# Starting the large SBUF tiles of a gated attention and ternary FFN kernel on multiples of 2048 bytes

## The reference

```python
x = x + tanh(g_xattn[0]) * xattn(layernorm(x), ctx_1024, ctx_1024, Wq, Wk, Wv, Wo, bo)
x = x + tanh(g_ffn[0]) * ffn(layernorm(x), w1_w, w1_s, w2_w, w2_s, h1_w, h1_s, h2_w, h2_s, w3_w, w3_s)

# xattn: 16 heads of 16, causal mask, softmax, concat @ Wo.T + bo
# ffn, with tlin(x, w, s) = (x @ w.T) * s and ternary weights w:
h = silu(tlin(x, w1_w, w1_s)) * tlin(x, w2_w, w2_s)      # 256 -> 1024
h = gelu(tlin(h, h1_w, h1_s))                            # 1024 -> 1024
h = gelu(tlin(h, h2_w, h2_s))                            # 1024 -> 1024
return tlin(h, w3_w, w3_s)                               # 1024 -> 256
```

## Time and profile before

| | |
|---|---|
| median of three runs | 1804.46 us |
| profiled execution | 1806.88 us |
| its span, first to last instruction | 1804.8 us |
| TensorE busy (PE, share of the span) | 1730.7 us (96%) |
| TensorE weight loads (PEld) | 1465.8 us (81%) |
| VectorE, ScalarE, GpSimd busy | 73%, 72%, 61% |
| granted TensorE clock, mean | 0.985 of full speed |
| DMA | 231.37 MB, mean 128 GB/s |

### The profile page before, as it was taken

The page is one execution under the profiler, slowest core; times in us unless marked ns, Lnnn a source line. Parts: engine busy times, 40 slices in busy tenths (PEclk is TensorE's granted clock), DMA queues, the critical chain, the costliest instruction groups (busy, mean ns, idle before and its releaser), DMA issues.

```text
span 1804.8 us, 39555 instructions
## 1 busy us (share of the span) xinstructions
PE 1730.7 (96%) x11014; PEld 1465.8 (81%) x11014; DVE 1321.6 (73%) x2803; ACT 1306.7 (72%) x3014; POOL 1106.8 (61%) x1646
## 2 busy tenths in 40 slices
PE   3399999999999999999999999999999999999998
PEld 2288888888888888888888888888888888888876
DVE  5767777777777777777777777777778777777764
ACT  3477777777777777777778777778777777777764
POOL 4666566567556567656567656656655656755652
PEclk8699999999999999999999999999999999999999
DMA  9944545544455544445554454554445554445420
GB/s 288 242 108 109 131 128 142 141 111 116 122 134 134 139 121 113 120 128 134 139 129 114 114 131 128 145 136 113 114 129 132 137 139 114 114 121 134 117 59 7
DMA packets 370970, 231.37 MB, mean 128 GB/s; under 512 B 283136, under 2 KB 340736, under 8 KB 369408
## 3 DMA queue, kind: packets, MB, share of 16 engines
q1 hardware_dynamic: 368784, 219.23, 47.7%
q10 hardware_dynamic: 2160, 11.81, 1.9%
HBM read 113.53 MB, written 41.94 MB: 86 GB/s over the span
## 4 chain that ended last, share of the span: by engine, by line
PE 91%; issue 2%; DMA 2%; POOL 2%; ACT 1%; DVE 1%; SPq 1%; POOLq 0%; DVEq 0%; ACTq 0%
PE ffn L976 71%; PE work L916 12%; PE s_bank L951 3%; PE pv L967 3%; PE work L1056 2%; DMA pT<-p_parts 1%; POOL p_parts L468 1%; POOL p_parts L466 1%; DMA aw<-in_attn_w 0%; DMA q<-q_saved 0%; POOL hb L513 0%; ACT probs L821 0%; SPq L360 0%; SPq L356 0%; POOL ha L508 0%
## 5 line engine op out<-in xcount | busy, mean ns | idle before, releaser
L976 PE MATMUL ffn<-hb,W 128*128 128x512 f32 x2048 | 512.2, 402 | 1.4 <-POOL hb L513 1.4
L976 PE MATMUL ffn<-ha,W 128*128 128x512 f32 x2048 | 492.1, 397 | 0.8 <-POOL ha L508 0.8
L658 DVE TENSOR_REDUCE full<-ffn 128x256 f32<-128x512 f32 x512 | 349.5, 688 | 194.1 <-PE ffn L976 194.1
L976 PEld LDWEIGHTS ffn<-ha,W 128*128 128x128 f32 x2048 | 379.4, 188 | 90.6 <-POOL ha L508 1.7
L976 PEld LDWEIGHTS ffn<-hb,W 128*128 128x128 f32 x2048 | 377.6, 188 | 86.3 <-POOL hb L513 2.3
L821 ACT ACTIVATE probs<-probs,exp_bias 128x128 f32<-128x128 f32 x1024 | 320.4, 390 | 50.8 <-POOL exp_bias L476 49.7
L468 POOL TENSOR_TENSOR p_parts<-probs,p_parts 128x512 f16<-128x512 f32 x256 | 300.4, 1173 | 20.5
L513 POOL TENSOR_TENSOR hb<-full,hb 128x256 fp32r<-128x256 f32 x256 | 187.3, 737 | 122.3 <-ACT full L839 116.5
L976 PE MATMUL ffn<-x2T_hi,W 128*128 128x256 f32 x1024 | 258.5, 287 | 1.4 <-DVE x2T_lo L754 0.9
L839 ACT ACTIVATE full<-full,cols 128x256 f32<-128x256 f32 x512 | 253.1, 494 | 0.0
L976 PE MATMUL ffn<-x2T_lo,W 128*128 128x256 f32 x1024 | 252.9, 284 | 0.0
(11 more groups left out here) (82 smaller groups left out, 2341.1 us busy)
## 6 DMA issues: line engine op xcount, KB each, us to landing
k<-k_saved SPq DMA_DIRECT2D x256, 128.0 KB, 2.8
q<-q_saved SPq DMA_DIRECT2D x256, 128.0 KB, 2.8
k_saved<-k_parts SPq DMA_DIRECT2D x32, 512.0 KB, 3.2
q_saved<-q_parts SPq DMA_DIRECT2D x32, 512.0 KB, 3.1
wnat<-in_ffn_w ACTq DMA_DIRECT2D x11, 1024.0 KB, 7.5
xT<-in_x_T SPq DMA_DIRECT2D x32, 256.0 KB, 3.3
cT<-in_ctx_T SPq DMA_DIRECT2D x32, 256.0 KB, 3.4
x_in<-in_x SPq DMA_DIRECT2D x32, 256.0 KB, 3.7
```

What stands on the lines that cost most here:

```text
L658: dve.tensor_reduce(full[:, m % 4], src[:].rearrange("p (a t) -> p t a", a=2), AX_X, ALU.add).then_inc(done, 1)
L976: return pe.matmul(dst, w, h, **flags)
```

## The change

All small tiles (statistics, biases, constants, and `vs`, which is 3136 bytes) are allocated first, then a filler `to_boundary` that nothing reads or writes, then the large tiles in their old order. The scratch region shrinks from 8192 to 4096 bytes. Scratch 4096, constants 128, small tiles 8800 and filler 1312 come to 14336 = 7 x 2048, and since all large tiles have sizes that are multiples of 2048, each of the tiles in the table above then starts on a multiple of 2048. The last byte moves from 228064 to 225280. No instruction, operand shape, wait, or order on any engine changes; only addresses in SBUF do.

```diff
+TO_BOUNDARY = 328
-        W = sb("W", [P, W_COLS], F32R)
-        aw = sb("aw", [P, 4, KE, E])
-        wq, wk, wv, woT = (aw[:, i] for i in range(4))
         ident = sb("ident", [P, P])
         causal = sb("causal", [P, P])
...
-        x_in = sb("x_in", [P, ROWS, E])
         stats = sb("stats", [P, ROWS, 6])
         moments = sb("moments", [P, ROWS, 2])
         var_eps = sb("var_eps", [P, ROWS])
         rstd = sb("rstd", [P, ROWS])
+        vs = sb("vs", [P, ROWS, H, VCOLS], BF16)
+        negmax = sb("negmax", [P, PSLOTS, 4])
+        exp_bias = sb("exp_bias", [P, PSLOTS, 4])
+        head_sum = sb("head_sum", [P, 2, PAIR, D])
+        rden = sb("rden", [P, ROWS, H])
...
+        wait_holder = sb("wait_holder", [P, 1])
+
+        to_boundary = sb("to_boundary", [P, TO_BOUNDARY])
+
+        W = sb("W", [P, W_COLS], F32R)
+        aw = sb("aw", [P, 4, KE, E])
+        wq, wk, wv, woT = (aw[:, i] for i in range(4))
+        x_in = sb("x_in", [P, ROWS, E])
         xres = sb("xres", [P, ROWS, E])
         xT = sb("xT", [P, KE, TOK])
         cT = sb("cT", [P, KE, TOK])
...
-    nc = bacc.Bacc("TRN2", target_bir_lowering=False, num_devices=1, dynamic_dma_scratch_size=8192)
+    nc = bacc.Bacc("TRN2", target_bir_lowering=False, num_devices=1, dynamic_dma_scratch_size=4096)
```

More of the change, by code:

```diff
@@ L99, in sem @@
             return ctx.enter_context(nc.semaphore(name))
-        W = sb("W", [P, W_COLS], F32R)
-        aw = sb("aw", [P, 4, KE, E])
-        wq, wk, wv, woT = (aw[:, i] for i in range(4))
+        COPIES = 4
+        PSLOTS = 4
+        TSLOTS = 2
         ident = sb("ident", [P, P])
@@ L128, in program @@
         rstd = sb("rstd", [P, ROWS])
+        vs = sb("vs", [P, ROWS, H, VCOLS], BF16)
[3 more added lines that the diff above has]
+        rden = sb("rden", [P, ROWS, H])
+        stats2 = sb("stats2", [P, ROWS, 6])
+        moments2 = sb("moments2", [P, ROWS, 2])
+        var_eps2 = sb("var_eps2", [P, ROWS])
+        rstd2 = sb("rstd2", [P, ROWS])
+        wait_holder = sb("wait_holder", [P, 1])
[4 more added lines that the diff above has]
+        x_in = sb("x_in", [P, ROWS, E])
         xres = sb("xres", [P, ROWS, E])
@@ L131, in program @@
         cT = sb("cT", [P, KE, TOK])
-        COPIES = 4
         q_parts = sb("q_parts", [P, 2, ROWS, KE, P], F32R)
@@ L139, in program @@
         k_saved = nc.dram_tensor("k_saved", [2, ROWS, P, KE * P], F32, kind="Internal").ap()
-        vs = sb("vs", [P, ROWS, H, VCOLS], BF16)
         v_rest = sb("v_rest", [P, ROWS, E])
-        PSLOTS = 4
         probs = sb("probs", [P, PSLOTS, 4, P])
-        negmax = sb("negmax", [P, PSLOTS, 4])
-        exp_bias = sb("exp_bias", [P, PSLOTS, 4])
         p_parts = sb("p_parts", [P, 2, 2, 4, P], F16)
-        TSLOTS = 2
         pT = sb("pT", [P, TSLOTS, 2, 4, P], F16)
-        head_sum = sb("head_sum", [P, 2, PAIR, D])
-        rden = sb("rden", [P, ROWS, H])
         heads = sb("heads", [P, ROWS, E])
@@ L154, in program @@
         x1_prev = sb("x1_prev", [P, ROWS, E])
[L155 to L158, removed]
         x2n = sb("x2n", [P, ROWS, E])
-        wait_holder = sb("wait_holder", [P, 1])
         x2T_hi = sb("x2T_hi", [P, KE, TOK], F32R)
```

## The result

The changed kernel takes 1791.35 us in the median of four runs (1788.92 to 1793.29), the kernel before 1805.5 us in the median of four (1802.91 to 1808.18). The ratio is 0.992, with a 95% interval of 0.9901 to 0.9939: faster by 0.8%. The forecast was no difference, 1804.5 us.

A forecast was written before the change was run, and what follows sets the result against it. Blocks were taken as bound by matmul count times start distance, after a prologue mostly on DMA. All terms were 0 (0 + 0 + 0 + 0), leaving the unchanged median, 1804.5 us; range 1780 to 1813.

The forecast's parts named there:

- The regimes: Whole kernel: a prologue of 89.4 us, then 31 or so blocks timed by matmul count times distance between starts.
- rival B: Matmuls: moving stream gets faster through in-step reads or rows not crossing 2048; 19.5 us gained, 1785 us; chance 0.23.
- A: Whole kernel: nothing hangs on the address, 1804.5 us (1801 to 1808); 0.55 together with the change not doing what it says.
- the place of the matmul operands: Matmuls in the blocks: new operand addresses cost 0, bounded by 19.5 us gained and 18.5 us lost.
- all four places: L2 weight loads at four starting remainders: 186 to 192 ns all, so a crossing slice costs under 1 ns per matmul.
- The crossing of a multiple of 2048: Moving rows of L1, kt 0 against kt 1: medians within 4 ns, so crossing was taken as 0.
- The scores: 256-column matmuls already in step before the change: 117.5 ns, like L4 and at most 2 ns faster than L1.
- the 20 ns: 512-column matmuls of L2 and L3: unexplained excess, 233.3 against 213.3 ns; 82 us if all went, given little chance.
- C: L2 and L3: slower because all streams start in step and compete; 18.5 us lost, 1823 us; chance 0.16.
- DMA: Six DMA pieces on the prologue's chain, 33.7 us: address effect taken as 0, bounded at 2.7 us to either side.
- The rule of the Trainium skill: Prologue DMA: 256-byte transactions begin at multiples of 256; aligned tiles might shorten the prologue by about 3 us.
- Scratch, other engines, instructions: Smaller scratch region, moved tiles of engines with slack in the blocks, and unchanged instruction counts: each cost 0.

The follow-up runs named there:

- e3: Changed kernel with all large tiles, W too, starting 736 bytes past a multiple of 2048, in step with each other; 1787.89 us, ratio 0.9902 to the kernel before.
- e5: Kernel before with a 1440-byte filler ahead of wnat, ha and hb, putting them in step with W, and scratch 4096 bytes; 1791.57 us, ratio 0.9918.
- e1: Changed kernel with ha and hb rows on multiples of 2048, W, aw and the other large tiles 128 bytes past one; 1805.7 us, ratio to before 1.0005.
- e2: Changed kernel with ha and hb (and wnat, wlow) 736 bytes past a multiple of 2048, other large tiles on one; 1808.09 us, ratio to before 1.0012.
- e6: Kernel before with the scratch region at 4096 bytes and nothing else changed; 1806.48 us, ratio 1.0002.
- e14: Kernel before with p_parts and pT alone put on a multiple of 2048, scratch 4096 bytes; 1804.04 us, ratio 0.9978.
- e8: Changed kernel with k4 and x2T at 288, ha at 128, hb at 256, W, aw and q4 at 0; 1788.94 us, ratio to before 0.9916.

## Why the prediction was wrong

**The regimes held.** The blocks are bound by the distance between matmuls and the prologue mostly by DMA, and what changed is in these two places. The lever was named (0.5 ns per FFN matmul is 3.6 us), and so was rival B's mechanism, reads that start in step. Its price of 19.5 us stands against 17.7 us measured in the blocks. The measured 1791.35 us lies within the stated 1780 to 1813, but there it belongs to B, which had 0.23; the forecast itself was A's.

**The step that failed** is the choice of 0 for "the place of the matmul operands". The runs showed 6.1 ns less for each matmul of L2 and 4.9 for L3 once moving row and weight slice start in step (e3 and e5 against e1, e2 and e6), 17.7 us in the blocks. The 0 was read from rows that could not show the effect:
- The weight loads at "all four places" (128, 640, 1152, 1664) differ by 512 bytes, which is two whole periods of 256. They were four samples of one offset. So was the evenness of 233.1 to 233.8 ns: every L2 and L3 matmul before the change has an offset of 736 - 128, which is 96 modulo 256. A constant distance was taken as a sign that addresses don't matter; it was the sign that the address relation never varied.
- The crossing of a multiple of 2048 was tested between kt 0 and kt 1 of L1, 1024 bytes apart, again whole periods. The answer (0) was right, and e3 shows it, but it was the wrong question. One reading in it is wrong: `W` as the moving operand of L4 does cross. Its slices are 1024 bytes and start at 128 and 1152, and the second reaches 2176. They only add another pair a whole number of periods apart.
- The scores were read as the one kind that is in step and gains nothing, and this was carried to 512 columns. The table shows that the two widths answer differently: in step is the best for 512 columns and, with 96, the slowest measured for L1. The argument "the scores keep almost all of the excess" compared unlike shapes. How the scores keep 117.8 ns before and 119.2 after, in step both times, isn't explained; they stand in pairs between other kinds.

**What spoke for B and was weighed too little**: the 20 ns by which 233.3 is above the prediction's 213.3, on 4096 matmuls. 6 ns of them went.

**B's price was right in sum and partly by luck.** It had L1 at 1.9 ns less and L2, L3 at 3.8 ns less. L1 gained nothing, L4 lost 1.4 ns (117.9 to 119.3) and the scores as much, while L2 and L3 gained 6.1 and 4.9 ns. By these means that is 22.5 us gained and about 3 lost, some 2 us more than the blocks show; the means leave out the distances at the ends of the pieces. Of its two mechanisms e3 excludes the one by rows that don't cross a multiple of 2048.

**C, slower because in step**, has a true part: 256 columns at L4 and in the scores do lose. 1.4 ns on 1536 matmuls is about 2 us.

**DMA** was bounded at 2.7 us to either side. The prologue's own scatter of 84 to 102 us is far wider than that; the bound was sized from one profile. In the first comparison the prologue was 5.3 us longer, outside the bound, and the median prologue was 4 to 5 us longer in all three sets.

**The rule of the Trainium skill** on 256-byte transactions holds for the transposes (3.1 to 2.7 us). The estimate made from it, a prologue 3 us shorter, did not come in the changed kernel. In e14 something of that size did (a median of 87.0 us against 90.8 in its set), but that run does not isolate the rule as the cause.

**Scratch, other engines, instructions**: 0, as said. e6 shows the first; the other two were not tested by themselves.

## What to carry to other kernels

Where matmuls of the same shape run back to back and take longer than their columns, look at the start address of the moving row less that of the weight slice, modulo 256 bytes, and try two or three offsets with a filler; one filler of 1440 bytes was worth 0.8% here (e5). Measure each width by itself, since 512 and 256 columns had different best offsets. Don't take evenness over addresses as independence from them before checking that the addresses differ in the bits that may count: steps of 512 and 2048 bytes hide a period of 256. A difference of one execution's prologue is worth little where DMA queues compete; compare the period of a loop, which repeats to 0.02 us.

## What the runs showed of the hardware

- The place of the weights and that of the moving operand of fp32r matmuls do not act apart: with the same shapes, 512 columns go at 227 to 229 ns with an offset of 0 or 64 and at 233 to 234 ns at 32, 96, 128, 160, 192 and 224 bytes. 256 bytes apart L3 goes as at 0 (e8). The Trainium skill ("TensorE: Matmul & The Clock Gate", section "Step-by-step: what each phase is for") says that loading the next tile's weights does not steal read bandwidth from the running matmul. Here the distance hangs on the relative address of the two, which speaks against reads that are wholly independent. Which read gives way to which, and by what mechanism, was not shown.
- In step, the weight loads of L1 take 192 ns in the median, and 188 where they are 96 bytes off (before); those of L2 take 188 at either.
- Plain fp32 matmuls of 256 columns (L916) keep a mean distance of 215.5 to 216.1 ns in every layout tried.
- A multiple of 2048 bytes in SBUF has no visible effect on the matmuls (e3 against the changed kernel: 11.00 us for 48 in both).
